# A broadcast load split off and asked for earlier: the cumulated sums of a Mamba-2 chunk, in a fused mixer and FFN kernel

## What is computed

```
A_cs = jnp.cumsum(A, axis=-1)
Lmat = jnp.exp(_segsum(A))               # exp(A_cs[l] - A_cs[s]) for l >= s, else 0
Y_diag = jnp.einsum('bcln,bcsn,bhcls,bcshp->bclhp', Cm, Bm, Lmat, X)
...
Y_off = jnp.einsum('bchpn,bcln,bhcl->bclhp', states, Cm, jnp.exp(A_cs))
y = (Y_diag + Y_off) + xh * D
y = y * silu(z)
y = y * rsqrt(mean(y * y) + EPS) * norm_w   # then the projection w_out
```

## Time and profile before

| | |
|---|---|
| median of 3 runs | 993.62 us (991.27 to 995.96) |
| profiled execution | 995.9 us, its span 994.1 us |
| TensorE busy | 937.7 us, 94% of the span |
| VectorE busy | 578.0 us, 58% |
| ScalarE busy | 352.4 us, 35% |
| GpSimd busy | 341.2 us, 34% |
| mean share of the DMA engines | q1 36.2%, q10 9.1% |

### The profile page before, as it was taken

The page is one execution under the profiler, slowest core; times in us unless marked ns, Lnnn a source line. Parts: engine busy times, 40 slices in busy tenths (PEclk is TensorE's granted clock), DMA queues, the critical chain, the costliest instruction groups (busy, mean ns, idle before and its releaser), DMA issues.

```text
span 994.1 us, 13243 instructions
## 1 busy us (share of the span) xinstructions
PE 937.7 (94%) x4960; PEld 468.5 (47%) x4960; DVE 578.0 (58%) x919; ACT 352.4 (35%) x537; POOL 341.2 (34%) x372
## 2 busy tenths in 40 slices
PE   4798878999899999999999999999999999999997
PEld 2343334555344445555545445555545445555543
DVE  5776377788452666666442766575542766575421
ACT  5584744543332344232221433232221433232200
POOL 0323242756010202856410203765510203766310
PEclk9899998999999999999999999999999999999999
DMA  9589553755422534354321535355321535254123
GB/s 333 215 290 355 173 180 109 250 177 174 152 92 85 172 104 148 120 159 136 99 73 55 183 105 161 106 148 143 91 75 53 184 105 158 65 148 149 43 76 95
DMA packets 80815, 142.64 MB, mean 143 GB/s; under 512 B 8048, under 2 KB 20976, under 8 KB 78704
## 3 DMA queue, kind: packets, MB, share of 16 engines
q1 hardware_dynamic: 61536, 113.79, 36.2%
q10 hardware_dynamic: 19216, 28.01, 9.1%
HBM read 115.82 MB, written 25.95 MB: 143 GB/s over the span
## 4 chain that ended last, share of the span: by engine, by line
PE 77%; DVE 9%; ACT 4%; issue 4%; DMA 3%; POOL 3%; ACTq 0%; SPq 0%; DVEq 0%; POOLq 0%
PE ps L572 50%; PE ps L777 17%; PE ps L742 2%; PE ps L734 2%; DMA arena<-cs_rows 2%; DVE arena L1165 2%; PE ps L728 2%; DVE arena L1116 1%; PE ps L697 1%; PE ps L714 1%; ACT arena L865 1%; POOL arena L1364 1%; POOL arena L1352 1%; DMA w_mid<-arena 1%; DVE arena L1186 1%
## 5 line engine op out<-in xcount | busy, mean ns | idle before, releaser
L572 PE MATMUL ps<-xh,arena 128*128 128x512 f16 x1600 | 498.4, 385 | 25.3 <-DVE arena L1181 8.5
L572 PE MATMUL ps<-xl,arena 128*128 128x512 f16 x800 | 308.0, 385 | 0.0
L572 PEld LDWEIGHTS ps<-xh,arena 128*128 128x128 f16 x1600 | 160.5, 100 | 220.2 <-issue 23.1
L777 PE MATMUL ps<-arena 128*128 128x512 f16 x768 | 171.1, 379 | 0.0
L1337 POOL TENSOR_TENSOR arena<-arena 128x512 f16<-128x512 f32 x64 | 78.4, 1227 | 225.9 <-ACT arena L917 225.9
L1352 POOL TENSOR_TENSOR arena<-arena 128x2048 f32<-128x2048 f32 x16 | 58.6, 3665 | 227.3 <-DMA arena<-cs_rows 227.3
L572 PEld LDWEIGHTS ps<-xl,arena 128*128 128x128 f16 x800 | 79.1, 99 | 91.1 <-issue 6.9
L1165 DVE SCALAR_TENSOR_TENSOR arena<-ps,cw,arena 128x511 f32<-128x511 f32 (+2 forms) x120 | 89.4, 747 | 49.4 <-ACT arena L907 47.5
L777 PEld LDWEIGHTS ps<-arena 128*128 128x128 f16 x768 | 74.4, 98 | 91.3 <-issue 5.7
L917 ACT ACTIVATE arena<-arena 128x512 f16<-128x512 f32 x64 | 40.4, 631 | 188.7 <-DVE arena L1186 188.7
L572 PE MATMUL ps<-wo_hi,arena 128*128 128x512 f16 x256 | 78.7, 379 | 0.1
(11 more groups left out here) (165 smaller groups left out, 1096.6 us busy)
## 6 DMA issues: line engine op xcount, KB each, us to landing
arena<-w_parts SPq DMA_DIRECT2D x198, 256.0 KB, 2.7
w_parts<-arena SPq DMA_DIRECT2D x66, 256.0 KB, 2.9
arena<-cs_rows ACTq DMA_DIRECT2D x16, 1024.0 KB, 6.1
arena<-w SPq DMA_DIRECT2D x8, 1024.0 KB, 8.8
arena<-w SPq DMA_DIRECT2D x32, 256.0 KB, 3.6
arena<-ecs_rows ACTq DMA_DIRECT2D x24, 256.0 KB, 7.6
arena<-w SPq DMA_DIRECT2D x8, 512.0 KB, 6.0
w_mid<-arena SPq DMA_DIRECT2D x16, 256.0 KB, 2.2
```

The source lines that it names most:

```text
L572: ins = nc.tensor.matmul(out_ap, lhs(i, a), rhs(i, c), start=(i == 0 and s == 0), stop=(i == n - 1 and s == 2))
L777: ins = nc.tensor.matmul(bank(t), hw[a][:, i, t * P:(t + 1) * P], w2s[i % W2R][:, d, :], start=(i == 0 and s == 0), stop=(i == JF - 1 and ...
```

## The change

The load of `csbc` becomes an entry `L` of its own, for chunks 1 to 3, at tiles 3, 9 and 17 (batch 0: 3, 9 and 16). `E` keeps its places, and there ScalarE still asks for `ecsb`. Chunk 0's `E` still asks for `csbc` itself. The waits of the `csbc` load stay: `d_cst` (the sums are in DRAM) and `esub_ok` of the chunk before (GpSimd has read the buffer). GpSimd's, DVE's and TensorE's code is the same.

```
-STEP_FIRST = {"T": (3, 8, 17, 26), "E": (None, 7, 14, 22), ...
+STEP_FIRST = {"L": (None, 3, 9, 16), "T": (3, 8, 17, 26), "E": (None, 7, 14, 22), ...
 STEP_AT = {
...
     "R": (8, 16, 24, 35),
+    "L": (None, 3, 9, 17),
     "E": (None, 6, 14, 22),
...
-                    elif kind == "E":
+                    elif kind == "L" or (kind == "E" and c == 0):
                         if b == 0 and c == 0:
...
                         act.wait_ge(d_cst, (b + 1) * 32)
                         act.wait_ge(esub_ok.sem, esub_ok.at(b, c - 1))
                         act.dma_start(csbc.rearrange("p h l -> p (h l)"),
                                       cs_rows[b, c].rearrange("h l -> (h l)").partition_broadcast(P)).then_inc(d_csbc, 16)
-                        if c > 0:
-                            act.wait_ge(t1_ok.sem, t1_ok.at(b, c - 2))
-                            for r in range(2):
...
+                    elif kind == "E":
+                        act.wait_ge(d_cst, (b + 1) * 32)
+                        act.wait_ge(t1_ok.sem, t1_ok.at(b, c - 2))
+                        for r in range(2):
+                            act.dma_start(ecsb[HD * r:HD * r + HD, :].rearrange("p (q l) -> p q l", q=QE),
+                                          ecs_rows[b, c].rearrange("(q r) l -> r q l", r=2)[r].partition_broadcast(HD)).then_inc(d_ecsb, 16)
```

More of the change, by code:

```diff
@@ L52 @@
             [("H", j, at) for j, at in enumerate((30, 31, 32, 33, 34, 35, 35, 38, 39, 40, 41, 42, 43, 44, 45, 46))])
-STEP_FIRST = {"T": (3, 8, 17, 26), "E": (None, 7, 14, 22), "X": (4, 11, 18, 29), "Y": (7, 14, 22, 32), "N": (9, 16, 24, 34), "Q": (9, 16, 24, 34),
+STEP_FIRST = {"L": (None, 3, 9, 16), "T": (3, 8, 17, 26), "E": (None, 7, 14, 22), "X": (4, 11, 18, 29), "Y": (7, 14, 22, 32), "N": (9, 16, 24, 34), "Q": (9, 16, 24, 34),
               "V": (11, 18, 26, 36), "ROW": (12, 19, 27, 37), "W": (14, 20, 28, 38)}
@@ L984, in _ @@
                                       cs_rows[b, c].rearrange("h l -> (h l)").partition_broadcast(P)).then_inc(d_csbc, 16)
-                        if c > 0:
-                            act.wait_ge(t1_ok.sem, t1_ok.at(b, c - 2))
-                            for r in range(2):
-                                act.dma_start(ecsb[HD * r:HD * r + HD, :].rearrange("p (q l) -> p q l", q=QE),
-                                              ecs_rows[b, c].rearrange("(q r) l -> r q l", r=2)[r].partition_broadcast(HD)).then_inc(d_ecsb, 16)
+                    elif kind == "E":
[4 more added lines that the diff above has]
+                                          ecs_rows[b, c].rearrange("(q r) l -> r q l", r=2)[r].partition_broadcast(HD)).then_inc(d_ecsb, 16)
                     elif kind == "T":
```

## The result

The changed kernel takes 1006.94 us, the median of four runs (1005.61 to 1008.52), beside 994.79 (991.27 to 997.29, four runs) for the kernel before: a ratio of 1.0125, 95% interval 1.0089 to 1.0162. It is slower by 12 us. The profiled execution took 1008.5 us, 1.6 above the median, and its span is 1006.7.

A forecast was written before the change was run, and what follows sets the result against it. From batch 1 on TensorE's own work was taken to bound the kernel, batch 0 being bound by DVE and ScalarE. -3.2 + 10.8 + 2 = +9.6 us on the median 993.6 gave 1003 us, range 989 to 1008.

The forecast's parts named there:

- rival 1: At `Y`: the gate runs beside the subtraction undelayed, the wait goes, nothing comes back; 986.4 to 990.4 us; chance 0.17.
- the second: At the gate and `N`: exclusion real but mostly hidden, stops fall to +4, less 3.2; 993 to 997 us; chance 0.17.
- The third: In batch 0: the early 1 MB load delays TensorE by meeting weight stores or loads; +15, 1009 us; chance 0.06.
- The gain: Batches 1 to 3: TensorE's two waits at L734 for GpSimd go; -3.2 us, bounds 0 and -3.2.
- The exclusion: Behind `Y`: the gate, starting second, stands until GpSimd's subtraction ends, then needs 1.2 us; some 2.9 us late.
- The stops at `N`: Batches 1 to 3: TensorE waits for the late squares behind `Y` of chunks 1 and 2, 1.6 us each.
- The small terms: Per batch: 0.2 us from chunk 0's `Y`, and 0.2 where chunk 2's transposes wait for a state sum.
- Batches 1 to 3 together: Stops and small waits of 3.6 us per batch, +10.8 in all, with -3.2 for L734's waits.
- Batch 0: Bound by DVE and ScalarE: gate put back by up to 2.4 us, weight split unblocked; +2 net, bounds -4 and +7.
- 998 to 1008 by its bounds: Whole time: the range given to the forecast itself, with chance 0.60.

The follow-up runs named there:

- e1: The changed kernel, with GpSimd also waiting for the gate of the chunk before ahead of its subtraction (chunks 1 to 3); 994.74 us beside 994.31 before.
- e3: The changed kernel, with GpSimd's subtraction cut into four instructions of 128x512; 992.18 us beside 994.31 for the kernel before.
- e5: The changed kernel, with GpSimd also waiting for its chunk's `ecsb` loads before subtracting (chunks 1 to 3): load early, start late; 994.25 us beside 993.69 before.
- e2: The changed kernel, with the sum ahead of the gate written back to PSUM and read there by the gate; 994.51 us beside 994.31 before.
- e4: The changed kernel, with batch 0's loads put back to the old tiles 7, 14 and 22; 1000.56 us beside 994.31 for the kernel before.
- e8: The changed kernel, with the subtraction in quarters and batch 0's loads at their old places; 989.36 us beside 993.69 before, ratio 0.9933.

## Why the prediction was right

The forecast was 1003.0 (989 to 1008), slower with 0.64, and 1006.9 was measured. Of its rivals, the first (the gate runs beside the subtraction) and the second (the exclusion is hidden) both fell with six waits at L754. The third (the early load collides) fell with e1, e3 and e5, which have the early load and lose nothing by it in batches 1 to 3; in batch 0 each loss that was followed up ends at an exclusion or at a queue, none at a DMA. Step by step:

- **The gain**, -3.2 us by the two waits of L734. Measured -4.0: the rest in e1 and e3, which have no new stop, less that of before. The waits are idle time of TensorE alone; the stretch of a batch says a little more.
- **The exclusion.** Right in kind and in size. L1274 was put 2.9 us late, ending 1.2 us after the subtraction, with bounds of 0.55 and 1.28; it ended 1.09 after, 2.7 us late. Order (e1), operand (e2) and hold (e3) each switch it off, so it is shown, not argued. The median of L1274, forecast as near 4 us, is 3.57: chunk 0 begins its gate 1.1 us into the subtraction in place of 0.7, and chunk 3, with no subtraction behind its `Y`, keeps 1285 ns, as does one more gate of batch 0.
- **The stops at `N`**, 1.6 us each, six times. They are there, six, and nowhere else. TensorE's row has 1.26 us for each and its weight load 1.76; the matmuls' ends are modelled, so the lengths of the batches decide. The cost of all stops is the rest of the change less that of e1: 674.6 - 663.4 = 11.2 us, where the forecast had 10.8. The small terms are there too: 0.28 us at the transposes, for 0.2 (the row names no engine, but the state sum L1264 ended 0.09 us earlier, at 891.23); and a weight load that stands 0.40 us for L1278 at `V` of chunk 0, for 0.2.
- **Batches 1 to 3 together**: forecast -3.2 + 10.8 = +7.6, measured +7.2 in the profile; e4, which has nothing else of the change, gives +7.4 by its ratio and +6.3 by the medians.
- **Batch 0** is the term that was mis-sized: +2, with bounds of -4 and +7, and measured +5.4 in the profile (5 to 5.6 from the medians). The step that failed is the one that set the old block of a split (2.4 us) against new delays of the gate alone. Both terms came: L1118 takes 2.2 us less between the first two `Y` (6.9 for 9.1 us busy), and the gate of chunk 2 takes 3.57 us, which with shorter splits beside it makes +0.8 in that stretch. The missing one is the other VectorE instructions with both tensors in SBUF that stand where the subtraction now starts: the pair L1241 at chunk 0 (4.77 us for 1.41) and, above all, two splits behind `Y` of chunk 1. The rows of before had this place: splits at 181.97 and 183.23, and the subtraction at 183.56, 1.56 us after GpSimd was free. They could not have said for sure that the first split loses, for it began 0.03 us before GpSimd was free; that the second stands inside an earlier subtraction they did show. I read one of the three subtractions of batch 0 and did not go through the other two.

In all, 7.2 + 5.4 = 12.6 us by the profile, for 9.6 forecast. The 3 us between are batch 0's. That 1006.9 lies inside 989 to 1008 is owed to the bound of +7 for batch 0, not to its middle. Two figures of the working are loose: "998 to 1008 by its bounds" moves batch 0's term alone (all bounds together reach from 986 to 1014), and the middle of rival 1's 986.4 to 990.4 is 988.4, not 989.

## What to carry to other kernels

A long idle time on GpSimd may be what keeps VectorE fast: before a GpSimd instruction is started earlier, look in the timeline for each VectorE instruction with both tensors in SBUF that runs in the hole, at every place where it occurs, and give each the rest of GpSimd's instruction as a delay. If TensorE's slack behind it is shorter than that delay, the time gets longer although GpSimd waits 62 us less for its loads. The remedy is not to give up the early load but to shorten the hold (quarters), to order the pair by a semaphore, or to leave one operand in PSUM. In this kernel each of them gave the loss back (e3, e1, e2), and only with the old places in batch 0 besides (e8) was the result better than before.

## What the runs showed of the hardware beyond the forecast

- The hold lasts for one instruction and is given up between two of the same kind. With GpSimd's queue full of quarters of 1.04 us, the gate still got in behind one of them and took 1.44 us.
- The exclusion goes round: the marker on one column behind the subtraction takes 1.05 us (885.81), until the gate is through; behind a subtraction with no gate waiting it takes 0.20 (e1, 878.60). It is the earlier trace rows's L1372 again, as part of every pair.
- A start 0.01 us earlier decides for the whole instruction: a split of 0.75 us became 4.14. Where both engines set out from the same instruction, so narrow a race came out the same way in five kernels.
- The one that stood needs nearly its whole length once it gets in: 1.09 us of 1.28 for the gate; the split ended 0.54 us after the subtraction (186.55 and 186.01), of its 0.75.
- The same kernel's batch 0 is not the same from one execution to the next: runs of the kernel before go from 989 to 1001 us, those of e1 from 993 to 997, and e8 has two of eight that are 4 to 7 us under the others, while the three later batches together take 663.4 to 663.7 us in four kernels and 674.6 in four others. Which instruction wins each of batch 0's races is part of that, and TensorE's granted clock goes with it: from `Y` of chunk 0 to `Y` of chunk 1 it is 0.85 to 0.96 in the twelve profiles, while the three later batches have 1.00. In e8's lucky execution this stretch took 36.92 us at 0.95 (40.5 us at 0.92 before). What of the spread is cause and what is effect was not measured.
